# Running part of a shared expert inside the channel-mix steps of a float32 AdaLN, RWKV and mixture-of-experts kernel

## The reference

```python
sa, ca, ga, sb, cb, gb = modulation(silu(c) @ wmod)     # one row of 512 each per batch
h = layernorm(x) * (1 + ca) + sa
hl = layernorm(h, ln1_g, ln1_b); hp = shift(hl)         # the row before
r = sigmoid(mix(mu_r) @ Wr.T); k = mix(mu_k) @ Wk.T; v = mix(mu_v) @ Wv.T
x2 = h + (r * sigmoid_like(u + k) * v) @ Wout.T         # time-mix adds h
h2 = layernorm(x2, ln2_g, ln2_b)
r2 = sigmoid(mix(mu_r2) @ Wr2.T); k2 = square(relu(mix(mu_k2) @ Wk2.T))
x = x + ga * (x2 + r2 * (k2 @ Wv2.T))                   # channel-mix
h3 = layernorm(x) * (1 + cb) + sb
shared = (silu(h3 @ Wsg.T) * (h3 @ Wsu.T)) @ Wsd.T      # 704 hidden
scores = softmax(h3 @ Wr.T)                             # 8 experts, the best 2 of each row
routed = sum of score * ((silu(h3 @ Wg[e].T) * (h3 @ Wu[e].T)) @ Wd[e].T)   # 352 hidden each
out = x + gb * (routed + shared)
```

## Time and profile before

| what | value |
|---|---|
| median of 3 runs | 1896.31 us (1895.73 to 1900.86) |
| span of the profiled execution | 1895.5 us |
| PE busy | 1742.5 us, 92% of the span |
| DVE busy | 1312.1 us, 69% |
| ACT busy | 707.1 us, 37% |
| POOL busy | 619.4 us, 33% |
| mean granted TensorE clock | 0.950 of 2.4 GHz |
| HBM traffic | 351 MB, 185 GB/s over the span |

### The profile page before, as it was taken

The page is one execution under the profiler, slowest core; times in us unless marked ns, Lnnn a source line. Parts: engine busy times, 40 slices in busy tenths (PEclk is TensorE's granted clock), DMA queues, the critical chain, the costliest instruction groups (busy, mean ns, idle before and its releaser), DMA issues.

```text
span 1895.5 us, 29657 instructions
## 1 busy us (share of the span) xinstructions
PE 1742.5 (92%) x9060; PEld 1509.1 (80%) x9060; DVE 1312.1 (69%) x2333; ACT 707.1 (37%) x1118; POOL 619.4 (33%) x755
## 2 busy tenths in 40 slices
PE   4599999998899899997779999999999999999997
PEld 0488888886677777776678998999999999988886
DVE  4898999983798888886632227666666666655555
ACT  2344444442443434343211115454545454522222
POOL 0343333322577777776216420000000000034442
PEclk8699999999888888888798999999999999999999
DMA  8333343333855454543448735767676767666553
GB/s 332 101 116 120 120 120 120 120 99 116 299 170 183 172 190 166 187 161 128 139 167 285 260 111 199 248 228 251 228 253 225 256 221 254 229 198 178 182 181 101
DMA packets 147870, 351.39 MB, mean 185 GB/s; under 512 B 20793, under 2 KB 20793, under 8 KB 142321
## 3 DMA queue, kind: packets, MB, share of 16 engines
q1 hardware_dynamic: 117136, 263.26, 41.7%
q0 software_dynamic: 19456, 67.12, 10.8%
q10 hardware_dynamic: 11232, 20.45, 2.8%
HBM read 225.95 MB, written 124.83 MB: 185 GB/s over the span
## 4 chain that ended last, share of the span: by engine, by line
PE 72%; DVE 16%; issue 5%; DMA 3%; ACT 2%; POOL 1%; DVEq 1%; SPq 0%; ACTq 0%; POOLq 0%
PE bank L451 17%; PE bank L453 17%; PE bank L452 17%; DVE mix L1345 5%; PE bank L1828 5%; PE bank L1830 5%; PE bank L1829 5%; PE bank L462 3%; PE bank L1804 2%; DVE xh L1330 2%; DMA stage<-in_w_k 1%; DVE raw L1630 1%; DVE h_hl L1400 1%; PE bank L1758 1%; DVE raw L1625 1%
## 5 line engine op out<-in xcount | busy, mean ns | idle before, releaser
L451 PE MATMUL bank<-gu_hi,ex_x_hl 128*128 128x352 f32 x1136 | 381.6, 336 | 24.2 <-DMA ex_x_hl<-h_turned 22.3
L453 PE MATMUL bank<-gu_hi,ex_x_hl 128*128 128x352 f32 x1136 | 370.0, 326 | 0.0
L452 PE MATMUL bank<-gu_lo,ex_x_hl 128*128 128x352 f32 x1136 | 367.3, 323 | 0.0
L1541 DVE TENSOR_TENSOR hid<-bank,sg_t 128x352 f32<-128x352 f32 x142 | 74.5, 525 | 298.3 <-ACT sg_t L1071 294.5
L882 POOL DMA_DIRECT2D ex_x_hl<-h_turned x32 | 18.4, 575 | 691.1 <-PE bank L453 659.9
L451 PEld LDWEIGHTS bank<-gu_hi,ex_x_hl 128*128 128x128 f32 x1136 | 215.5, 190 | 25.2 <-issue 14.5
L1071 ACT ACTIVATE sg_t<-bank 128x352 f32<-128x352 f32 x142 | 65.9, 464 | 417.7 <-PE bank L453 390.9
L452 PEld LDWEIGHTS bank<-gu_lo,ex_x_hl 128*128 128x128 f32 x1136 | 215.6, 190 | 0.0
L453 PEld LDWEIGHTS bank<-gu_hi,ex_x_hl 128*128 128x128 f32 x1136 | 214.7, 189 | 0.0
L1828 PE MATMUL bank<-dn_hi,hid_hi 128*128 128x512 f32 x426 | 169.0, 397 | 9.7 <-DVE hid_lo L1545 9.1
L1830 PE MATMUL bank<-dn_hi,hid_lo 128*128 128x512 f32 x426 | 168.7, 396 | 0.0
(11 more groups left out here) (215 smaller groups left out, 4051.8 us busy)
## 6 DMA issues: line engine op xcount, KB each, us to landing
raw<-in_ex_gu SPq DMA_DIRECT2D x39, 1408.0 KB, 6.6
expert_in_rows<-zero_rows SPq DMA_DIRECT2D x32, 624.0 KB
raw<-in_ex_dn SPq DMA_DIRECT2D x39, 512.0 KB, 7.6
ex_x<-expert_in_rows SPq DMA_DIRECT2D x78, 256.0 KB, 2.7
expert_out_rows<-y_rows ACTq DMA_DIRECT2D x78, 256.0 KB, 2.8
h_rows<-h_t SPq DMA_DIRECT2D x64, 256.0 KB, 3.2
h_turned<-h_hl POOLq DMA_DIRECT2D x32, 512.0 KB, 4.4
ex_x_hl<-h_turned POOLq DMA_DIRECT2D x32, 512.0 KB
```

Source lines behind the costliest of these rows:

```text
L451: pe.matmul(acc, act_hi[i], w_hi[i], start=(i == 0), stop=False)
L452: pe.matmul(acc, act_hi[i], w_lo[i], start=False, stop=False)
L453: last = pe.matmul(acc, act_lo[i], w_hi[i], start=False, stop=(i == chunks - 1))
L1541: dve.tensor_tensor(hid[:, half, 0:F], PS_U[half][:, 0:F], sg_t[:], ALU.mult).then_inc(u_vec.sem_of["hid"], 1)
```

## The change

What it does, stage by stage:

- SBUF is laid out by hand (`Shelf`), so that the shared expert's weights fit beside the channel-mix's. They are loaded in step 0 and 1 of the channel-mix and split in its steps 1 to 5 (`shared_hi`, `shared_lo`).
- Time-mix: DVE adds h to the output product (`x2_of`, lag 3) and SP stores x2; `o_rows`, the stored output and POOL's `x2` are gone. SP loads h again in time-mix (`load_hin`) and x2 in channel-mix.
- Channel-mix: `tk` and `cv` move from the step after into the same step, the residual and h3 from two or three steps later to one, `t3` and the router from four to two; several ring buffers become single ones and banks are shared (`cv` writes k2's bank, `t3` writes `t2`'s, the logits share a bank with the gate's product). Each tile loads its 768 KB of modulation rows (`load_mod`). h3 turned is stored from the ACT queue.
- From step 6 to step 33 each channel-mix step also does one unit of the shared expert, 28 in all, tiles 0 to 13 (`FU` = 14, `LAG` = 6), with its own residual in DRAM (`load_rs`, `store_rs`).
- `EARLY` is then tiles 14 to 22, with routing in its units 0 to 5, `SC` = 4 scatter buffers, and the shared expert's loads on the ACT queue. SP then loads the 14 finished tiles' rows back before the routed rows.
- `LATE` is tiles 23 to 31; `combine` and `first_product` handle a pair of tiles in every unit.

The diff, cut to its core:

```diff
-SPLIT = NT // 2
-SC = 3
+FU = 14
+SPLIT = 23
+LAG = 6
+SC = 4
...
-EARLY = Part(0, SPLIT, 0, None)
+FUSED = Part(0, FU, 0, None)
+EARLY = Part(FU, SPLIT, 0, FUSED)
...
+def with_units(eng, lead, body):
+    sweep(eng, NT, lead, LAG + 2, body)
...
         # SP
-            sweep(sp, NT, *in_turn((later_ho, -5), (load_mod2, 0), (load_ahead, 1), (load_x2, 1), (store_xres, 2), (load_xr, 1), (store_h3, 3), (later_x2, -4)))
+            lead, _, channel_step = in_turn((load_mod, 0), (load_x2r, 0), (load_xr, 0), (load_shared, 0), (load_rs, LAG),
+                                            (store_xres, 1), (store_h3, 1), (later_x2, -4), (store_rs, LAG))
...
+            for n in range(2):
+                load_scattered(n)
+            for n in range(FU, FU + 2):
+                load_residual(n)
+            sp.wait_ge(*base_vec.done(FU - 1, "base"))
+            for n in range(2, SC):
+                load_scattered(n)
...
+            sp.wait_ge(route_done, 1)
+            for first in range(2):
+                load_expert(ROUTED.tile(first))
+            for n in range(SC, NT):
+                load_scattered(n)
+            sp.wait_ge(rs_out, 16 * FU)
+            for n in range(FU):
+                if n >= 2:
+                    sp.wait_ge(fb_in[n % 2], 16 * (n // 2))
+                sp.dma_start(base[:, n, :], xres_d[n * P:(n + 1) * P, :]).then_inc(fb_in[n % 2], 16)
...
         # POOL
-            sweep(pool, NT, *in_turn((diff_2, -1), (x3, 2), (rstd_3, 3), (rstd_2, -3), (gated, 2), (xres, 2), (x2, -4),
-                                     (store_turned, 5)))
+            lead, _, channel_step = in_turn((diff_2, -1), (x3, 1), (gated, 1), (xres, 1), (rstd_3, 1), (rstd_2, -3))
+            with_units(pool, lead, channel_step)
...
             for n in range(NT):
-                if n % SC == 0 and 4 + n // SC < SPLIT:
-                    load_turned(4 + n // SC)
                 pool.wait_ge(sc_in[n % SC], 16 * (n // SC) + 16)
...
         # ACT
-            sweep(act, NT, *in_turn((sr2_of, 0), (k2hi, 1), (h3hi, 4), (mix2_hi, -1), (k2_of, 0), (h2T_of, -2),
-                                    (first_gu0, 1), (first_gu1, 2)))
+            lead, _, channel_step = in_turn((sr2_of, 0), (k2_of, 0), (hidhi_of, LAG), (mix2_hi, -1), (silu_of, LAG),
+                                            (k2hi, 0), (h3hi, 2), (store_turned, 2), (h2T_of, -2), (shared_hi, 0),
+                                            (first_turned, 0))
...
         # DVE
+            def x2_of(t):
+                dve.wait_ge(*rw_pe.done(t.n, "out"))
+                dve.wait_ge(hin_in[t.p], 16 * t.half + 16)
+                dve.tensor_tensor(hin_t[:, t.p, :], PS_O[:], hin_t[:, t.p, :], ALU.add).then_inc(x2_vec.sem, 1)
...
-            sweep(dve, NT, *in_turn((pads, 1), (y_of, 2), (logits_out, 5), (first_col_2, -1), (stats_3, 3), (stats_2, -3), (moments_3, 3), (xhat_2, -2),
-                                    (moments_2, -3), (mixes_2, -1), (h3lo, 4), (k2lo, 1), (mix_lo_2, -1), (scaled_3, 3),
-                                    (h3_of, 3), (first_shared, 4)))
+            lead, _, channel_step = in_turn((logits_out, 3), (first_col_2, -1), (mixes_2, -1), (fused_hidlo, LAG),
+                                            (mix_lo_2, -1), (stats_3, 1), (moments_3, 1), (fused_hid, LAG), (k2lo, 0),
+                                            (h3lo, 2), (scaled_3, 1), (h3_of, 1), (stats_2, -3), (moments_2, -3),
+                                            (xhat_2, -2), (fused_base, LAG), (pads, 0), (shared_lo, 0), (y_of, 0))
...
-            ROUTING = {0: softmax_and_first, 1: second, 3: earlier_tiles, 4: padded_counts, 5: row_slots, 6: tile_experts}
+            ROUTING = {0: softmax_and_first, 1: second, 2: earlier_tiles, 3: padded_counts, 4: row_slots, 5: tile_experts}
...
+            for n in range(SPLIT, NT):
+                t = LATE.tile(n)
+                for half in range(2):
+                    before = LATE.before(t, half)
+                    hidlo(*before)
+                    hid_of(LATE, t, half)
...
+                    elif not half:
+                        base_of(LATE, n - 1)
...
+                    q = 2 * (n - SPLIT - 1) + half
+                    if 0 <= q < NT // 2 - 1:
+                        combine(q)
...
         # PE
-            sweep(pe, NT, *in_turn((r2, 0), (tk, 1), (t3, 4), (k2, 0), (t2, -2), (router, 4), (cv, 1)))
+            def fused_up(v):
...
+                    rows_turned(w.p)
...
+                rows_up(PS_G[0], 0, 1, v.p)
+                pe.wait_ge(*lg_vec.done(v.back(LAG - (LAG + 3)).n, "copied"))
+                rows_up(PS_U[0], F, 1, v.p).then_inc(u_pe.sem_of["up"], 1)
...
+            lead, _, channel_step = in_turn((r2, 0), (k2, 0), (fused_up, LAG), (tk, 0), (t3, 2), (fused_down, LAG),
+                                            (cv, 0), (router, 2), (t2, -2))
+            with_units(pe, lead, channel_step)
```

More of the change, by code:

```diff
@@ L8 @@
+import math
 from contextlib import ExitStack
@@ L133, in sweep_part, with one_by_one, in_fused @@
     sweep(eng, part.count, lead, lag, body, part.first)
+def one_by_one(part, lead, lag, body):
+    for n in range(part.first - lead, part.count + lag):
+        body(Tile(None, n, part.count, part.first))
+def with_units(eng, lead, body):
+    sweep(eng, NT, lead, LAG + 2, body)
+def in_fused(v):
+    return v.real() and (v.pair is not None or v.offset < 2 * FU)
 def in_turn(*stages):
@@ new lines, in build @@
+        hid = kept.put("hid", [P, 2, FK * P])
+        hid_hi = kept.put("hid_hi", [P, FK, P], F32R)
+        hid_lo = kept.put("hid_lo", [P, FK, P], F32R)
+        ex_x_hi, ex_x_lo = [x[:, 0] for x in ex_x_hl], [x[:, 1] for x in ex_x_hl]
+        third = Shelf(nc, w2_at)
+        raw = [third.put(f"raw{i}", [P, RAW]) for i in range(2)]
+        mod3 = third.put("mod3", [P, B, D])
+        sc_first = Shelf(nc, third.at).put("sc_first", [P, 2, D])
+        y_rows = third.put("y_rows", [P, 2, D])
@@ new lines, in build @@
+        sc_rows = [sc_first[:, 0, :], sc_first[:, 1, :], sc_second[:, 0, :], sc_second[:, 1, :]]
+        route = {name: temp.put("route_" + name, [P, NT, E]) for name in
+                 ("ex", "sc", "oh1", "oh2", "tmp", "both", "cur", "nxt", "pos")}
+        row = {name: temp.put("route_" + name, [P, NT, 1]) for name in ("mx", "sum", "rec", "pick", "s1", "s2")}
+        iota_e = temp.put("iota_e", [P, NT, E])
+        iota_ei = temp.put("iota_ei", [P, NT, E], I32)
+        count = {name: temp.put("route_" + name, [P, 1, E]) for name in ("total", "padded", "end", "end2", "start")}
@@ L1128, in routed_step @@
                         routed_x_hi(t, 1)
[L1129 to L1130 removed]
+                    hidhi_before(*ROUTED.before(t, half))
+                    silu(ROUTED.unit(t, half), bank_of(ROUTED, half))
+                    if t.only(NJ - 1):
+                        load_turned(LATE, SPLIT + half)
                     if t.back(1).real():
@@ L1165, in _ @@
-            sweep_part(act, LATE, 1, 1, late_step)
+            for n in range(SPLIT, NT):
+                t = LATE.tile(n)
+                for half in range(2):
+                    if n == SPLIT:
+                        expert_hi(Tile(None, NJ + 1, NJ + 2), half)
+                    hidhi_before(*LATE.before(t, half))
+                    silu(LATE.unit(t, half), bank_of(LATE, half))
+                    if half and n + 2 < NT:
+                        load_turned(LATE, n + 2)
+                    if n == SPLIT:
+                        store_y(ROUTED.last(), half)
+                    else:
+                        first_product(2 * (n - SPLIT - 1) + half)
@@ L1168, in _ @@
+            hidhi_before(LATE, LATE.last(), 1)
+            for q in range(2 * (NT - SPLIT - 1), NT // 2):
+                first_product(q)
         @block.vector
@@ L1445, in _ @@
+            with_units(dve, lead, channel_step)
             wait_a2(dve)
+            for i in range(2):
+                dve.memset(raw[i][F % P:P, RAW - D:RAW], 0.0).then_inc(raw_pad, 1)
             taken = [0]
@@ L1825, in down @@
                 pe.wait_ge(*u_vec.done(u, "hid_lo"))
-                start, stop = part is ROUTED or half == 0, part is ROUTED or half == 1
-                for c in range(FK):
-                    pe.matmul(PS_Y[:], hid_hi[:, c, :], dn_hi[w][:, c, :], start=start and c == 0, stop=False)
-                    pe.matmul(PS_Y[:], hid_hi[:, c, :], dn_lo[w][:, c, :], start=False, stop=False)
-                    last = pe.matmul(PS_Y[:], hid_lo[:, c, :], dn_hi[w][:, c, :], start=False, stop=stop and c == FK - 1)
-                last.then_inc(u_pe.sem_of["down"], 1)
+                rows_down(w, part is ROUTED or half == 0, part is ROUTED or half == 1)
             def turn_rows(t, half):
@@ L1870, in _ @@
             sweep_part(pe, ROUTED, 1, 1, routed_step)
-            def late_step(t):
-                if t.only(NT):
-                    turn_hid(LATE, LATE.last(), 1)
-                    down(LATE, LATE.last(), 1)
```

(4 more changed lines are left out.)

980 lines of the change are left out of this document (509 added, 471 removed).

## The result

The changed kernel takes **1908.07 us**, median of 4 runs (1906.57 to 1913.71), where the kernel before took 1896.82 in the same measurement: a ratio of 1.0066, interval 1.0045 to 1.0086. It is slower by 0.7%. I had forecast 1871 us, faster; the time lies inside my range of 1828 to 1912, and its sign is the other one.

The account below looks back on a forecast made before the run. It took neither PE nor DVE to be full in channel-mix, and PE to lack work after it. Terms +2, +113, -58 and -82 sum to -25 us on 1895.5: 1871 us, 8-in-10 range 1828 to 1912.

Parts of the forecast that it names:

- Early part: First early `up` to routed part: 165 us instead of 223, -58 us, set by scatters and loads; PE's work 118 us.
- First `up` to the route's end: Early part: the route's end releases POOL 43 us behind the first `up`, one unit earlier than the 49.5 before.
- Rows of the fifth tile: Early part: the fifth scatter tile's rows stand in SP's queue behind 4.2 MB of weights, 20 us.
- 28 tiles of scatters: Early part: with four buffers a scatter tile takes 2.7 us instead of 3.48, bounds 2.5 and 3.48.
- The hole of 45 us: Before the routed part: PE idle some 45 us waiting for routed rows; the largest new wait.
- Steps 0 to 5: Channel-mix steps without a shared unit: 16 us each (bounds 15 and 17.5) plus 2 for weight splits, 98 us.
- Late part: Late shared units with combines: 17 intervals of 7.3 us, first combine's wait +3, tail 14.4; 141.5 us, -82 us.
- The fused step: Channel-mix step with a shared unit: PE bounds it at 16.9 us (16.87 to 18.5), never idle, clock 1.00.
- the rival of the loop at 18.5 us: Fused steps: the loop through all engines bounds the step at 18.5 us, 42 us more, 1913 us; chance 0.2.
- the draining table switch: Fused steps: ACT's table switches drain, some 0.8 us for each of 28 steps, 1893 us; chance 0.1.
- The start: Time-mix to the first r2: `x2_of` on DVE hidden except at the end, +2 us.
- The rival of scatters at the rate of issue: Early part: 64 scatters at 1.26 us, residual loads at 2; routed part 25 us sooner, 1846 us; chance 0.2.

Follow-up runs that it names:

- e4: Changed kernel with ACT's part of shared tiles 16 to 19 in a loop over pairs, PE's code left straight: 1892.80 us (0.9990).
- e2: Changed kernel with the 14 residual loads moved behind SP's routed loop: 1879.53 us in set 1, 1909.33 us when run again unaltered on another chip.
- set 1: First of five sets of runs: four variants of the changed kernel on one chip, beside the kernel before; none of the four stalled.
- e1: Changed kernel with PE's shared tiles 16 to 21 in a loop over pairs instead of straight code: 1892.24 us (0.9986).
- f3: Changed kernel with residual loads behind the routed loop and 24 instead of 23 tiles before the routed part: 1912.54 us (1.0080).
- j1: i1 with 24 instead of 23 tiles before the routed part, still at most two tiles of scatters under way: 1876.32 us (0.9909).
- f1: Changed kernel with residual loads behind the routed loop and 25 instead of 23 tiles before the routed part: 1922.21 us (1.0126).
- a_again: The changed kernel, unaltered, run again in another set: 1907.70 us (1.0068).
- i1: Changed kernel, residual loads behind routed loop, expert weights after scatter tiles 16 and 18, scatters waiting for those two tiles back: 1885.90 us (0.9943).
- h2: f1 with PE's shared tiles 16 to 23 in a loop instead of straight code: 1922.47 us (1.0142).

## Why the forecast was wrong

**Early part: the step that failed.** "PE has 118 us of work" and the routed start set by the scatters alone, 165 us after the first `up`. The chain itself was right to 4 us: the routed rows were requested 160.8 us after that `up` (1200.81 - 1040.02), where I had 43 + 114 = 157. What I left out is that the scatters do something to the engines beside them. From the first `up` to the last early silu it took 186.8 us instead of the 118 or so that I gave to PE's work (e4, without the stall: 123.5). The last early silu came at 1226.85, in unstalled kernels near 1163; so the early units, with a cover of 45 us in hand, became the last to be ready. The price is the difference between e2's two runs, 30 us, where the moved loads count too; for the changed kernel itself it is some 15 us, against another chip: e4, the changed kernel but for ACT's loop, has 1892.8 in set 1, and its first routed silu at 1219.1 instead of 1235.7. So of the 26 us by which the stretch from the first `up` to the first routed silu is over its forecast, 16 are the stall; the other 10 are there in e4 too, whose scatters end 6 us later. None of my rivals had this mechanism. The trace of before could hint at it only by its absence. Its scatters ran at 1.92 us each, and PE was busy throughout (windows view of 1000 to 1106 us):

```profile
1000.00:1106.00 106.00, 106.00 (x595) 99.10 (x596) 27.92 (x48) 15.31 (x32) 58.94 (x65) 0.97 0.80 266
```

POOL's waits in that stretch say what held them back:

```profile
POOL ex_x_hl L882 <- PE bank L453: 21.3, 6, 4.4
POOL expert_in_rows L912 <- DMA sc_rows<-h_rows: 12.6, 5, 3.0
```

The turned load that stands in POOL's queue after every third tile waited for PE's `up`, so the scatters were tied to PE's own pace; their rows, the only thing that a fourth buffer helps, held them up less. I read that pace as something to be won, at 2.7 us a tile, and the change took the tie away together with the pauses.

**The pieces of the chain.** First `up` to the route's end: 48.0 us (1087.99), not 43. Rows of the fifth tile: 24.4 us behind it (1112.35), not 20. 28 tiles of scatters: 72.7 us, 2.6 a tile, forecast 2.7. That agreement is luck: I had scaled 3.48 us by three buffers over four, from a stretch that leaves out the longest pauses (the whole pace of before is 3.84 a tile), but POOL waits for no row after 1112 and only the issue, 1.26 us a scatter, bounds the changed kernel. The 14 residual loads: 21.1, not 25. Each is small, and they cancel. The hole of 45 us is there in e1 and e4, 45.0 and 45.1.

**Without the stall next to nothing would have been won.** e1 and e4 stand at 0.9986 (0.9974 to 0.9997) and 0.9990 (0.9978 to 1.0002), 2 to 3 us below the kernel before, where I had forecast 25. The rest of the miss is in these terms.
- *Steps 0 to 5*: 106.6 us (476.26 to 582.83), not 98. PE's waits from 480 to 592 us say why:

```profile
PE bank L507 <- DVE k_lo L1434: 22.1, 6, 4.2
PE bank L518 <- ACT k_t L1052: 8.8, 6, 1.5
```

  5.2 us a step behind the making and the split of k2, which now lie inside one step, and part of PE's work at the lower clock (0.85 granted on average above). My upper bound, 6 x 17.5 + 2 = 107, would have been the value to take.
- *Late part*: 149.6 from the first silu. From the first to the last hid it is 133.8 us, 7.9 an interval with the first combine's wait in it, not 7.3 (with my 3 us for that wait, 7.5):

```profile
1755.78 0.53 DVE L1507 TENSOR_TENSOR hid<-bank,sg_t 128x352 f32<-128x352 f32 x1 [2.34 <-ACT sg_t L1095]
...
1889.62 0.52 DVE L1507 TENSOR_TENSOR hid<-bank,sg_t 128x352 f32<-128x352 f32 x1
```

  hid_lo behind the combine was there as forecast (PE waits 12.2 us for it at seven places), and the first combine waited for its gather, 3.9 us against my 3. The runs with more early tiles show what I hadn't seen: 8 late tiles take 142.3 and 142.6 us (f3, j1) and 7 take 142.5 (f1). So below nine tiles the units no longer set this part; the gathers and combines are what is left, though no run takes them apart.
- *The route* as above: 5 us.

**What was right.** The fused step: 16.94 us (582.83 to 1006.39 over 25 steps), forecast 16.9, PE full and at 1.00. It stands or falls with these rows of one step, PE, DVE and ACT together:

```profile
786.74 0.48 PE L507 MATMUL bank<-w_r_hi,xm_hi 128*128 128x512 f32 x1
...
799.97 0.74 DVE L1458 SCALAR_TENSOR_TENSOR h_t<-xr_t,mv,mod_t 128x512 f32<-128x512 f32 x1
...
802.29 0.51 DVE L1406 TENSOR_SCALAR xh<-x_t,mv,rstd 128x512 f32<-128x512 f32 x1
...
803.63 0.48 PE L507 MATMUL bank<-w_r_hi,xm_hi 128*128 128x512 f32 x1
...
812.12 1.06 ACT L1037 ACTIVATE xm_hi<-mix 128x1024 fp32r<-128x1024 f32 x1 [0.97 <-DVE mix L1421]
...
813.20 1.28 ACT L1095 ACT_TABLE_LOAD   x1
...
814.49 0.47 ACT L1095 ACTIVATE sg_t<-bank 128x352 f32<-128x352 f32 x1
```

The operation that took 1.78 us beside POOL's addition takes 0.74 here, with POOL idle from 799.44 to 802.55, and `xhat_2`, 1.40 there, 0.51. So the rival of the loop at 18.5 us didn't come. Nor did that of the draining table switch: the copy ends at 813.18, the load begins at 813.20, silu 1.29 us later. The Trainium skill (ScalarE: Activation LUTs, What ACT_TABLE_LOAD costs) has 1.38 us more for each; no row here shows it. The start came out 2 us earlier, not later, so `x2_of` on DVE cost nothing that shows. The rival of scatters at the rate of issue had the pace right (1.28 us on two chips against 1.26) and the outcome wrong for the same reason as the forecast.

## What to carry to other kernels

When an edit lets a queue of indirect DMAs run at the rate of its issue, ask what the old pace protected: here a wait on the scatters two tiles back ended them 6 us later than in the kernels that were spared (1196.1 against 1190.5 in e2 of set 1) and took away a stall that costs more, 30 us in e2. A wait whose releaser the profile can't name, together with an engine that stops inside a product, suggests that the trouble isn't in the program's dependencies; vary the neighbour's pace before rewriting the engine's code. And when a kernel and its variants differ all at once, run the unchanged one again beside them: four variants had "cured" a stall that their chip didn't have.

## What the hardware showed

- Beside scatters of 128 rows issued every 1.28 to 1.32 us by GpSimd, ScalarE waited 61 to 74 us in all for products of TensorE that were done, on three chips, with DMA at 295 to 303 GB/s; at 1.74 to 1.77 us each, with 293 to 301 GB/s, it didn't. In the 70 us from 1112 on PE was busy 17 us (a_again) against 51.5 (i1). At 1.40 to 1.42 us each, on one chip, it didn't either.
- On one chip, two tiles of scatters under way gave 1876.3 us and no stall, three gave 1895.8 and waits of 69.6 us.
- The DMA engines' busy share was 0.88 or more in every run that stalled and 0.87 or less in every one that didn't. No run varies it by itself.
- The same kernel took 1879.5 us on one chip and 1909.3 on another, while the kernel before differed by 0.9 us between them.
- Fetching instructions isn't needed for the stall: 54.9 us of wait with no packet of instructions in 115 us (h2).
- Through what path a scatter delays what TensorE has finished isn't shown by any run here. Every execution on record has its span recorded, so no run tells either whether recording plays a part.
